# Picks per attention chunk 5, 5, 5, 4 in place of 5, 5, 5, 5, with a gathered column more in every fourth chunk

## The reference

```
h      = (x @ W.T)                       # per node, 2 heads of 16 (third layer: 1 of 32)
logits = leaky_relu(a_s[src] + a_d[dst]) # a_s, a_d: dot products of h with two vectors
m      = segment_max(logits, dst);  ex = exp(logits - m[dst])
out    = segment_sum(ex / segment_sum(ex, dst)[dst] * h[src], dst) + bias
```

## Time and profile before

| | us |
|---|---|
| median of 3 timed runs | 15026.58 (15022.28 to 15072.07) |
| the profiled execution's own time | 14966.27 |
| its span, first to last instruction | 14964.5 |
| attention layers, first to last reduction | 303.8 to 10744.8 |

### The profile page before, as it was taken

The page is one execution under the profiler, slowest core; times in us unless marked ns, Lnnn a source line. Parts: engine busy times, 40 slices in busy tenths (PEclk is TensorE's granted clock), DMA queues, the critical chain, the costliest instruction groups (busy, mean ns, idle before and its releaser), DMA issues.

```text
span 14964.5 us, 207967 instructions
## 1 busy us (share of the span) xinstructions
PE 12397.7 (83%) x54859; PEld 10572.3 (71%) x54859; DVE 8446.2 (56%) x16145; ACT 7971.3 (53%) x11216; POOL 9100.7 (61%) x9606
## 2 busy tenths in 40 slices
PE   3899998995699999999299999999758888888884
PEld 2788887884588888788288878888636666666663
DVE  5555555554355555555255555555536666666665
ACT  3666666663466666666166666666434444444442
POOL 5666666666666666666666666666566556556554
PEclk9999999997799999999599999999879999999996
DMA  2333333332122222222122222222123333333332
GB/s 85 79 81 79 84 80 80 80 81 56 47 48 49 48 48 48 50 48 49 33 47 49 49 48 49 48 48 48 44 78 97 98 95 100 94 97 97 97 97 52
DMA packets 911781, 1004.21 MB, mean 67 GB/s; under 512 B 343926, under 2 KB 690196, under 8 KB 911444
## 3 DMA queue, kind: packets, MB, share of 16 engines
q1 hardware_dynamic: 575588, 753.18, 17.3%
q0 software_dynamic: 307888, 198.91, 9.1%
q10 hardware_dynamic: 28224, 51.21, 0.9%
HBM read 648.97 MB, written 353.40 MB: 67 GB/s over the span
## 4 chain that ended last, share of the span: by engine, by line
PE 71%; issue 16%; DVE 5%; another core or an unknown queue 4%; ACT 2%; POOL 1%; DMA 0%; SPq 0%; DVEq 0%; ACTq 0%; POOLq 0%
PE bank L924 56%; PE bank L921 10%; PE wide L924 2%; PE bank L961 1%; POOL nodebuf L755 1%; DVE u_sb L1702 1%; PE bank L952 1%; ACT nodebuf L1084 1%; PE wide L952 1%; DVE adf L1666 1%; DVE s_b L1692 1%; ACT oh_x L1091 1%; DVE wide L1662 0%; ACT x_nm L1001 0%
## 5 line engine op out<-in xcount | busy, mean ns | idle before, releaser
L924 PE MATMUL bank<-tab,oh 128*128 128x448 f32 x35280 | 8109.8, 375 | 870.8 <-issue 864.8
L824 POOL DMA_INDIRECT g<-table,idx x6435 | 6088.7, 946 | 3811.1 <-issue 1804.8
L924 PEld LDWEIGHTS bank<-tab,oh 128*128 128x128 f32 x35280 | 6812.7, 194 | 1781.2 <-issue 1129.2
L1091 ACT ACTIVATE oh<-nodebuf 128x896 fp32r<-128x896 bf16 x2940 | 2653.2, 943 | 3872.0 <-remote 2357.7
L1084 ACT ACTIVATE nodebuf<-nodebuf,key_at 128x640 bf16<-128x640 f16 (+1 forms) x5488 | 3890.1, 789 | 902.5 <-DMA nodebuf<-keys_m 778.1
L1575 DVE TENSOR_REDUCE g<-bank 128x32 f32<-128x480 f32 x2940 | 1812.9, 648 | 3852.6 <-remote 2537.9
L824 POOL DMA_INDIRECT g<-tablex,idx x2341 | 2208.8, 944 | 1512.9 <-issue 689.5
L921 PE MATMUL bank<-tab,oh 128*128 128x480 f32 x5880 | 1826.7, 391 | 210.1 <-issue 167.9
L924 PE MATMUL bank<-tab,oh_x 128*128 128x448 f32 x7056 | 1635.4, 379 | 160.4 <-issue 159.7
L924 PEld LDWEIGHTS bank<-tab,oh_x 128*128 128x128 f32 x7056 | 1384.4, 197 | 331.1 <-issue 196.2
L921 PEld LDWEIGHTS bank<-tab,oh 128*128 128x128 f32 x5880 | 1139.6, 194 | 345.4 <-issue 206.9
(11 more groups left out here) (300 smaller groups left out, 7575.2 us busy)
## 6 DMA issues: line engine op xcount, KB each, us to landing
state<-o_sb SPq DMA_DIRECT2D x585, 288.0 KB
g<-table,idx POOLq DMA_INDIRECT x6435
auxx<-wide SPq DMA_DIRECT2D x97, 1056.0 KB
xd_in<-auxx SPq DMA_DIRECT2D x194, 512.0 KB
nodebuf<-keys_g SPq DMA_DIRECT2D x588, 160.0 KB
nodebuf<-keys_g SPq DMA_DIRECT2D x588, 150.0 KB
xe_t<-in_edge_attr SPq DMA_DIRECT2D x196, 256.0 KB
vmax<-o_sb ACTq DMA_DIRECT2D x194, 256.0 KB
```

The source lines that it names most:

```text
L824: eng.indirect_dma_start(o, None, t[:, :], bass.IndirectOffsetOnAxis(ap=idx[k][:, j:j + 1], axis=0)).then_inc(e_g[k][j // (W // 2)], 16)
L924: last = eng.matmul(o[:, 0:FR], hot[:, b, at], tab[:, a, b * FR:(b + 1) * FR], start=False, stop=(b == LB - 1 and a == 1))
L1091: eng.activation(hot[:, :, at], far[:, :, at], ACT.Relu, scale=-2.0, bias=1.0).then_inc(E["oh"], 1)
```

## The change

`PICKS` is (5, 5, 5, 4): chunk k = 3 of each iteration has four picks and gathers its column 4, so twelve columns. `GROUP` becomes 19, which five banks don't divide; so pick c uses bank c, and a new function `used` gives the count of the last earlier pick with the same c, for the bank's and the one-hot's wait. For c = 4 of chunk 0 that is the pick of chunk 2. In `gather_edges` nothing is edited, but its waits are worked out from `PICKS` and `nth`.

```diff
-PICKS = (5, 5, 5, 5)
+PICKS = (5, 5, 5, 4)
 SA = max(PICKS)
 AHEAD = [sum(PICKS[:k]) for k in range(NB)]
 GROUP = sum(PICKS)
 RING = 5
-assert GROUP % RING == 0 and len(PICKS) == NB
+assert SA == RING and len(PICKS) == NB
...
+def used(layer, i, k, c):
+
+    kp = max(x for x in range(k - NB, k) if PICKS[x % NB] > c)
+    return nth(layer, i - (kp < 0), kp % NB, c + 1)
...
             def picks(layer, i, k):
                 for c in range(PICKS[k]):
-                    done = nth(layer, i, k, c + 1)
-                    pick(bank[(AHEAD[k] + c) % RING][:, 0:FB], oh, c, done, done - RING)
+                    pick(bank[c][:, 0:FB], oh, c, nth(layer, i, k, c + 1), used(layer, i, k, c))
...
                 def hots(i, k):
                     for c in range(PICKS[k]):
-                        kp = (k - 1) % NB
-                        same = min(c + 1, PICKS[kp])
-                        one_hot(oh, c, i * NB + (layer * NC + k + 1), nth(layer, i - (k == 0), kp, same))
+                        one_hot(oh, c, i * NB + (layer * NC + k + 1), used(layer, i, k, c))
...
-                        v_.tensor_reduce(view(g[k], c * F, [[1, F]]), view(bank[(AHEAD[k] + c) % RING], 0, [[1, F], [F, TB]]), AX.X, ALU.max)\
+                        v_.tensor_reduce(view(g[k], c * F, [[1, F]]), view(bank[c], 0, [[1, F], [F, TB]]), AX.X, ALU.max)\
```

## The result

The changed kernel takes 15216.6 us (median of 4 runs, 15210.41 to 15233.78), the kernel before beside it 15040.31 us (4 runs, 15022.28 to 15072.07): ratio 1.0117, 95% interval 1.0096 to 1.0138. That is 176 us more; 138 us more had been forecast. The profiled execution took 15233.78 us (span 15231.9). Against the profiled one of before that is 268 us, of which 47 us lie in the edge network, where nothing was edited (first to last pick's reduction there 3703 us before, 3750 us after), so the timed runs are the ones to go by. The profile after has 2793 reductions and 6582 gathers, as the edit requires.

A forecast was written before the change was run, and what follows sets the result against it. A loop of GpSimd's gather bursts and TensorE's stops was taken as the bound; 147 x 1.0 = +147 us, less 9 us at layer ends, +138 us, gave 15165 us; range 14920 to 15290, likeliest 15080 to 15240.

The forecast's parts named there:

- The loop of two engines: Attention layers: TensorE stops while GpSimd issues gathers, GpSimd then waits for picks; 7.6 us of each 67.2 us iteration stands still.
- the account of busy time, gaps and waits: GpSimd, per iteration: 41.5 us busy, 12.3 us gaps, 13.3 us waits, sum 67.2 us.
- The additional gather: GpSimd, chunk k = 3: one gather more per iteration, 0.944 + 0.323 = 1.27 us at the most, 0 at the least.
- The removed pick: TensorE, chunk k = 3: 2.88 us less per iteration goes into longer stops; VectorE's and ScalarE's shares worth nothing.
- The number and length of the waits: GpSimd's waits for picks: 5.62 or 5.91 an iteration at about 2.26 us, 0.7 or 1.2 us more; 1.0 taken.
- The closer deadlines: Banks and one-hots reused after three picks, not four, following the short chunk: 0 to 0.3 us an iteration, 0 taken.
- The rule of the Trainium skill: SBUF engine and DMA ports are disjoint, neither slows the other; by it stops have another cause, the pick's time is won.
- (a): Rival: TensorE is the bound, its stops belong to its instructions; 423 to 494 us less, chance 0.16.
- (b): Rival: seven gathers opened at once save GpSimd one wait an iteration, 147 us less at full effect; chance 0.16.
- (c): Rival: closer deadlines bite, VectorE waits for chunk 3's gathers; 0.5 to 1 us an iteration on top; chance 0.08.

The follow-up runs named there:

- the kernel with an edit in each layer: Kernel before with only columns 14 and 15 gathered (layer one), no inner marks (two), 64 partitions' rows gathered (three): 14879.44 us, ratio 0.9946.
- layer two: In the last run, kernel before with rows of 16 partitions gathered for 128 in attention layer two: 67.0 us an iteration there; whole run 14554.09 us.

## Why the prediction was right

**What bounds the kernel.** The loop of two engines held where the kernel was measured. The strongest evidence are layers one and two of the kernel with an edit in each layer: stops gone with the gathers, and 8 us more an iteration when only waits were taken away. A gather fewer was worth 198 us, a shortened pick 36 us. Two parts of the prediction's reading don't hold as they stand. "While gathers are being issued" is too wide: TensorE runs on for some 11 us of a burst, and most short bursts don't stop it at all. And the account of busy time, gaps and waits, which "closes" for any engine, does not make GpSimd's busy time the bound: 4.6 us less of it in an iteration won 0.1 us. TensorE's stops were put at 7.6 us as what was left over; the rows give 366.5 / 44.66 = 8.2 us, which leaves 1.4 us, and not 2.0, for the lower clock.

**The additional gather.** Costed at 1.27 us; 190 us over 147 iterations, 1.29 us, in the pair that differs by the gather and the marks, 1.35 us in the gather taken from the kernel before. The size is right, the reason only in part: the price was made of issue and gap, and layer two shows that a gather with a cheaper issue costs as much. That issue and gap (1.27 us) come near to what a gather adds behind a burst (1.4 us) is luck.

**The removed pick.** Costed at nothing; it gave back 26 to 36 us, 0.2 us an iteration. No run takes VectorE's and ScalarE's smaller shares away by themselves.

**The number and length of the waits.** This was the open term. Their number fell with the picks, 5.70 for 5.91 (5.62 for a fall in proportion). Their mean grew from 2.26 to 2.37 us behind longer bursts. The forecast had taken 13.0 us an iteration for them, the middle of its two values; 13.5 came. This is the term that was sized too small, and it is the whole way from the 68.2 us forecast to the 68.7 us of the profile. These rows sort GpSimd's idle time by what ended it: "issue" takes in pauses of up to 5.3 us, and some "waits" are mere gaps of 0.30 us. Sorted by length, pauses of 1 us and more are 230 of 2.66 us before and 207 of 2.91 us after: 5.15 an iteration became 4.74, but in sum 13.7 us stayed 13.8. Fewer and longer pauses cancel, and what an iteration has more is the gather's 0.94 us and 0.5 us of gaps. The clock at 0.92 for 0.97 wasn't foreseen either. The account has no term for it, and whether it lengthens the waits isn't shown; it may, since GpSimd waits for picks, and behind the burst of thirteen they run at a granted clock of 0.50 (last but two in the row):

```profile
3029.00:3033.00 4.00, 2.82 (x5) 1.35 (x5) 3.83 (x8) 0.53 (x2) 1.88 (x2) 0.50 0.08 10
```

TensorE's stops, about 500 us in 3000 forecast, were 490.

**The closer deadlines** cost nothing here: no wait of a load for ScalarE or VectorE stands in the 3000 us. Without stops such waits do come, 62.6 us in 2500.

**The rule of the Trainium skill** (SBUF — State Buffer, "SBUF: two separate sides"). By this section of the Trainium skill a DMA and a compute operation can't slow each other. The runs bear out the row against the rule as it was used: gathers and TensorE's stops go together. But the stops don't go with the rows moved, as the layers with 64 and 16 partitions show, so they don't speak for a contest over ports either.

**The rivals.** (a), TensorE as the bound, is false for the regime measured, and true for the other, where the change makes the kernel 1.7% faster. The prediction had no word on that second regime; it rested on one execution. That the runs beside the result fell into the regime that the prediction had read is luck. (b) is seen in part: bursts of thirteen and fifteen came, and by length there are 4.7 pauses an iteration, but they are longer by as much. (c) didn't come.

**What stays open.** What a gather does to hold TensorE back, whether the late sight of finished picks has the same cause, whether another kind of DMA in bursts as long would do it too, and what decides between the regimes. The change of regime isn't the kernel's: the same one took 12680 us in one set and 14962 us in a later one on the same chip. No kernel was found that is the faster one in both: five picks throughout is better with stops, 5, 5, 5, 4 without them. More than five picks wasn't tried.

## What to carry to other kernels

When a busy engine stops for "issue", lay the other engines' timelines beside it and see with what its stops begin and end, whatever the busy shares say. Which engine's work counts is then shown by taking a unit of it away, not by adding up an engine's time: a gather less brought 1.35 us, cheaper gathers nothing. Before a unit of work is moved from one engine to another, price it at both ends by the period of the whole loop, in the regime without stops 2.88 us for a pick and 1.25 us for a gather; with stops a pick is worth 0.2 us and a gather 1.3 to 1.4 us. And take the time of the unchanged kernel again beside every experiment: here it showed that half of the experiments had run in another regime.

## What had not been expected of the hardware

- The same program ran in 12680 us or in 14803 to 15040 us, with an iteration of 57.6 or 67 us; the edge network differs too, 3072 us (first to last pick's reduction, kernel without inner marks) for 3703. GpSimd's issue of a gather was 0.944 us in both; TensorE's stops, 8.2 us an iteration, were there in one and absent in the other.
- In the regime with stops TensorE runs on for some 11 us of a burst of gathers; the stop then ends 12.9 us after the start of a burst of nine, and 1.4 us later for each further gather, whether a gather is issued every 1.25 us or every 1.14.
- An indirect DMA of 16 rows takes nearly as long to issue as one of 128: 0.840 for 0.944 us (64 rows: 0.903 us), with the same gap of 0.3 us behind it. A plain DMA of 128 rows of 128 bytes takes 0.537 us.
- Taking waits away can cost time: in the regime with stops a layer without GpSimd's four inner marks took 75.0 us an iteration for 67.1; in the other the marks made no difference (ratio 1.0000).
